# Filling a score operand stack in quarter-block portions, with the trailing attention stages one pair of steps closer

## The chip, the cores and the metric

The kernel runs on one core of one Trainium2 chip. The metric is the device time of one execution in microseconds (us). The kernel before takes 1998.75 us, the median of three runs (1997.51 to 2001.54).

## What is computed

Four layers of a Flamingo-like decoder in float32, on x of 8 x 256 tokens x 256 features, against a context of the same shape. Each layer is a gated cross-attention (16 heads of 16 features) followed by a gated feed-forward part; the latter differs from layer to layer (two dense ones in layer 0, eight experts with two chosen in layers 1 and 2, a quantised one with a convolution in layer 3). Cut to what matters here:

```
for l in range(4):
    x = x + tanh(g_xattn[l]) * xattn_l(norm(x), ctx)   # layer 0 with a mask of keys
    x = x + tanh(g_ffn[l]) * ffn_l(norm(x))
xattn: q, k, v = projections, heads of 16
       scores = q k^T / 4; attn = softmax(scores over keys); out = attn v
```

Only the attention of each layer is touched by the change.

## The kernel before

**Split operands.** To keep float32 accuracy, every query and key value is split into a high part and a low remainder. A score is the sum of three products, so the operands are stacked on partitions: `stack` holds, for each of two heads (partitions 0 and 64 on), three row blocks of 16 partitions: for the keys high, high, low; for the queries high, low, high. Partition 48 of each head holds one more row: ones for the keys, and for the queries the negated row maximum, so that the second score product comes out with the maximum already taken off. One slot of `stack` holds one block: one batch entry of 256 tokens, all eight pairs of heads. There are three slots (`SLOTS`) for eight blocks.

**How the stack is filled.** SyncE stores the split values of 512 tokens to the DRAM tensor `qk_parts` (`store_k`, `store_q`, three stores of 512 KB each, in the order of the row blocks), and GpSimd loads them back in stack form (`load_stack`: four loads of 48 x 8 x 256 values, 384 KB each, for one block: keys of two heads, queries of two heads). Both wait on counting semaphores: `k_out` and `q_out` say that a store has landed, `stack_in` of a slot that its loads have.

**The pipeline.** A step `t` is one pair of heads of one block; a turn `n` of the loops in `attend` is two steps (the code counts 32 turns as `QUADS`), so a block is four turns: block `b` begins with turn 4b. In turn n TensorE computes the natural scores of the turn (`scores_nat`, L792), VectorE takes their row maxima (`maximum`, L1709), and one turn later TensorE transposes the maxima (`max_rows`, L814), ScalarE copies them to `mt` (`take_rows`, L1294), and GpSimd writes them as a row into the stack by a small DMA (`put_rows`, L545). `KEY` turns after the natural scores TensorE computes the keyed scores (`scores_key`, L827) from stack and row, which ScalarE exponentiates (L1285); `TIMES_V` turns behind come the products with the values (L852), and `BACK` turns behind the transposes back (L865) and the divisions.

**What sets the order.** Every engine runs its program in order; there is no scheduler. In GpSimd's program the first three blocks are loaded ahead of the first turn, and `put_rows(l, n)` of turns 7, 11, 15, 19 and 23 is followed by the four loads of one later block. All these DMAs share GpSimd's queue and are served in the order in which they are issued. `mt` has two buffers, and ScalarE waits before it writes one again until the row written from it has landed:

```
if j >= 2:
    act.wait_ge(row_in[j % 2], 16 * (j // 2))
```

In TensorE's program the natural scores stand first in each turn, and the first of a block waits for the whole block; keyed scores, `max_rows`, `back` and `times_v` of that turn stand behind it:

```
if c == 0:
    loads = sum(x % SLOTS == b % SLOTS for x in range(B)) * l + b // SLOTS + 1
    pe.wait_ge(stack_in[b % SLOTS], 64 * loads + 16 * (l + 1))
```

Of the kernel before, what the change touches and what calls it, by code (L numbers as in the profile page):

```python
# [25 lines left out]
F32 = mybir.dt.float32  # L26
F32R = mybir.dt.float32r
# [8 lines left out]
P = 128  # L36
B, S, D = 8, 256, 256
# [13 lines left out]
STACK = 3 * DH + 1  # L51
MAXROW = 3 * DH
SLOTS = 3
KEY, TIMES_V, BACK = 4, 5, 6
PROJ_IN = {1: 48, 2: 80, 3: 128}
MASKED = -2.0 ** 100
MAGIC = 1.5 * 2.0 ** 23
# [36 lines left out]
def build(nc, io, upto=8):  # L94

    ctx = ExitStack()
    with ctx:
        def sb(name, shape, dt=F32, stack=ctx):
            return stack.enter_context(nc.sbuf_tensor(name, shape, dt))

        def sem(name, n=None):
            if n is None:
                return ctx.enter_context(nc.semaphore(name))
            return [ctx.enter_context(nc.semaphore(f"{name}{i}")) for i in range(n)]
# [48 lines left out]
        k_parts = sb("k_parts", [P, 2, 2, KC, 512], F32R, at)  # L153
        q_parts = sb("q_parts", [P, 2, 2, KC, 512], F32R, at)
        vpad = sb("vpad", [P, TILES, HEADS * (DH + 1) + 16], F32, at)
        mt = sb("mt", [8, 2, P], F32R, at)
        probs = sb("probs", [P, 4, 512], F32, at)
        pvs = sb("pvs", [P, 2, 256], F32, at)
        rc = sb("rc", [P, 2, 2, 4], F32, at)
# [1 line left out]
        def k_hi(g):  # L161
            return k_parts[:, g % 2, 0]

        def k_lo(g):
            return k_parts[:, g % 2, 1]

        def q_lo(g):
            return q_parts[:, g % 2, 0]

        def q_hi(g):  # L170
            return q_parts[:, g % 2, 1]
# [85 lines left out]
        xt = nc.dram_tensor("x_tokens", (T, D), F32, kind="Internal").ap()  # L257
        xs = nc.dram_tensor("xs_sorted", (NT * P, D), F32, kind="Internal").ap()
        ys = nc.dram_tensor("ys_sorted", (NT * P, D), F32, kind="Internal").ap()
        parts = nc.dram_tensor("qk_parts", (2, 2, MAXROW, PAIRS, T), F32, kind="Internal").ap()  # L260

        PS = ctx.enter_context(nc.psum_tensor("PS", [P, 8, 512], F32))

# [13 lines left out]
        qhi_done, qlo_done, v_done = sem("qhi_done"), sem("qlo_done"), sem("v_done")  # L277
        k_out, q_out = sem("k_out", 2), sem("q_out", 2)
        stack_in = sem("stack_in", SLOTS)
        mt_done, row_in = sem("mt_done"), sem("row_in", 2)  # L280
        nat_mm, max_done = sem("nat_mm"), sem("max_done")
        maxT_mm = sem("maxT_mm")
        sc_mm, exp_done = sem("sc_mm"), sem("exp_done")
# [46 lines left out]
        def stored(out, l, g):  # L330

            n = GROUPS * l + g
            return out[n % 2], 48 * (n // 2 + 1)

        def rows_of(n, r, g):

# [16 lines left out]
        def _(sp):  # L353
# [11 lines left out]
            def store_k(l, g):  # L365

                sp.wait_ge(khi_done, GROUPS * l + g + 1)
                sp.wait_ge(klo_done, GROUPS * l + g + 1)
                for r, part in enumerate((k_hi(g), k_hi(g), k_lo(g))):
                    sp.dma_start(rows_of(1, r, g), part.bitcast(F32)).then_inc(k_out[g % 2], 16)  # L370

            def store_q(l, g):

                sp.wait_ge(qhi_done, GROUPS * l + g + 1)
                sp.wait_ge(qlo_done, GROUPS * l + g + 1)
                for r, part in enumerate((q_hi(g), q_lo(g), q_hi(g))):
                    sp.dma_start(rows_of(0, r, g), part.bitcast(F32)).then_inc(q_out[g % 2], 16)

            def load_proj(l):
# [129 lines left out]
        def _(pool):  # L509
# [9 lines left out]
            def load_expert(l, e):  # L519
# [5 lines left out]
                nc.gpsimd.dma_start(wslot[:, slot, KC * h:2 * KC * h].rearrange("p (j d) -> p j d", d=D),  # L525
                                    io[f"W2_{l}"][e * h:(e + 1) * h, :].rearrange("(j p) d -> p j d", p=P)
                                    ).then_inc(w_in[slot], 16)
            def load_stack(l, b):

                if b >= SLOTS:  # L530
                    pool.wait_ge(sc_mm, 2 * STEPS * l + 2 * PAIRS * (b - SLOTS + 1))
                else:
                    nc.gpsimd.dma_start(stack[MAXROW:MAXROW + 65:64, b % SLOTS, 1].rearrange("p c n -> p (c n)"),
                                        io["ones_rows"]).then_inc(stack_in[b % SLOTS], 16)
                for n, out in ((1, k_out), (0, q_out)):
                    pool.wait_ge(*stored(out, l, b // 2))
                    for h in range(2):
                        nc.gpsimd.dma_start(stack[64 * h:64 * h + MAXROW, b % SLOTS, n],  # L538
                                            parts[n, h][:, :, b * S:(b + 1) * S]).then_inc(stack_in[b % SLOTS], 16)

            def put_rows(l, n):

                j, c, b = QUADS * l + n, 2 * n % PAIRS, 2 * n // PAIRS
                pool.wait_ge(mt_done, j + 1)
                nc.gpsimd.dma_start(stack[MAXROW:MAXROW + 65:64, b % SLOTS, 0, c:c + 2, :].rearrange("p c n -> p (c n)"),  # L545
                                    mt[:, j % 2, :]).then_inc(row_in[j % 2], 16)
            for l in lo_l:
                if l:

# [12 lines left out]
                if l == 0:  # L562

                    def make_mask(b):
                        pool.wait_ge(mask_in[b % 2], 32 * (b // 2 + 1))
                        nc.gpsimd.tensor_scalar(mask_b[:, b], stage_i[:, b % 2], 0.0, None, ALU.is_equal
                                                ).then_inc(mask_done, 1)
                    for g in range(GROUPS):

                        pool.wait_ge(khi_done, g + 1)  # L570
                        if g >= 2:
                            pool.wait_ge(*stored(k_out, 0, g - 2))
                        nc.gpsimd.tensor_tensor(k_lo(g), ctx_at(g), k_hi(g).bitcast(F32), ALU.subtract
                                                ).then_inc(klo_done, 1)
                        if g < 2:
                            make_mask(g)
                    load_stack(0, 0)
                    pool.wait_ge(v0_in, 16)
                    for g in range(GROUPS):
                        nc.gpsimd.tensor_copy(v_heads(4 * g, 4)[:, :, :, 0:DH],  # L580
                                              v_in[:, 4 * g:4 * g + 4, :].rearrange("p t (h d) -> p t h d", d=DH)
                                              ).then_inc(v_done, 1)
                else:
                    load_stack(l, 0)
                load_stack(l, 1)
                load_stack(l, 2)
                for n in range(QUADS):
                    if l == 0 and n % 2 == 1 and n // 2 + 2 < B:
                        make_mask(n // 2 + 2)
                    put_rows(l, n)  # L590
                    if n % 4 == 3 and n >= 7 and n // 4 + 2 < B:
                        load_stack(l, n // 4 + 2)
                if l == 3 and ffn(3):

                    pool.wait_ge(o_done, QUADS * 4)
# [75 lines left out]
        def _(pe):  # L671
# [102 lines left out]
            def scores_nat(l, t):  # L774

                s, b, c = STEPS * l + t, t // PAIRS, t % PAIRS
                if t == 0:
                    pe.wait_ge(qlo_done, GROUPS * (l + 1))
                    pe.wait_ge(klo_done, GROUPS * (l + 1))
                    if l:  # L780
                        pe.wait_ge(v_done, GROUPS * (l + 1))
                if c == 0:
                    loads = sum(x % SLOTS == b % SLOTS for x in range(B)) * l + b // SLOTS + 1
                    pe.wait_ge(stack_in[b % SLOTS], 64 * loads + 16 * (l + 1))
                if s:
                    pe.wait_ge(max_done, 2 * s - 1)
                q, kk = stack[:, b % SLOTS, 0, c], stack[:, b % SLOTS, 1, c]
                for qt in range(2):

                    for h in range(2):  # L790
                        rows = slice(64 * h, 64 * h + MAXROW)
                        mm = pe.matmul(PS[:, (2 * t + h) % 3, qt * S:(qt + 1) * S], q[rows, qt * P:(qt + 1) * P],  # L792
                                       kk[rows], start=(l > 0 or qt == 0), stop=(l > 0), skip_group_check=(l == 0))
                        if l and qt:
                            mm.then_inc(nat_mm, 1)
# [20 lines left out]
            def scores_key(l, t):  # L816

                s, b, c = STEPS * l + t, t // PAIRS, t % PAIRS
                j = s // 2
                pe.wait_ge(row_in[j % 2], 16 * (j // 2 + 1))  # L820
                if s:
                    pe.wait_ge(exp_done, 2 * s - 1)
                q, kk = stack[:, b % SLOTS, 0, c], stack[:, b % SLOTS, 1, c]
                for kt in range(2):
                    for h in range(2):
                        rows = slice(64 * h, 64 * h + STACK)
                        mm = pe.matmul(PS[:, 3 + (2 * t + h) % 3, kt * S:(kt + 1) * S], kk[rows, kt * P:(kt + 1) * P],  # L827
                                       q[rows], start=(l > 0 or kt == 0), stop=(l > 0), skip_group_check=(l == 0))
                        if l and kt:
                            mm.then_inc(sc_mm, 1)  # L830
# [367 lines left out]
        def _(act):  # L1198
# [89 lines left out]
            def take_rows(l, n):  # L1288

                j = QUADS * l + n  # L1290
                act.wait_ge(maxT_mm, j + 1)
                if j >= 2:
                    act.wait_ge(row_in[j % 2], 16 * (j // 2))
                nc.scalar.activation(mt[:, j % 2, :], PS[0:8, 6, S:S + P], ACT.Identity).then_inc(mt_done, 1)  # L1294

            def take_pv(l, n):

# [979 lines left out]
```

## Time and profile before

| | |
|---|---|
| median of three runs | 1998.75 us |
| the profiled execution | 1983.74 us |
| its span, first to last instruction | 1981.9 us |
| mean granted TensorE clock | 0.868 of full speed |
| TensorE busy | 1470.5 us, 74% |
| VectorE busy | 1083.2 us, 55% |
| ScalarE busy | 735.4 us, 37% |
| GpSimd busy | 544.0 us, 27% |

The profile is of one execution. Busy time is the union of an engine's instructions; the shares are averages over stages with different limits, so a stage must be looked at by itself. The four attention stages lie at about 56 to 255, 449 to 610, 1111 to 1268 and 1630 to 1802 us of the span. In rows of the time line the columns are start, duration, engine, line, operation and tiles, count, and in brackets how long the engine was idle before and what ended that.

### The profile page before, as it was taken

The numbers are of one execution on the slowest core, as the hardware profiler recorded it, in microseconds if no ns is written. First come the engines' busy times: TensorE is split into PE (matmuls) and PEld (weight loads), VectorE is DVE, ScalarE is ACT, GpSimd is POOL, SyncE is SP. The second block draws the span as 40 slices with busy tenths as digits, with TensorE's granted clock in tenths as the row PEclk, the third lists the DMA queues.
The fourth block names the chain that finished last, engine by engine and source line by source line (L and its number), as shares of the span: only waits on it lengthen the run. The fifth ranks groups of instructions, "written<-read, shape, count | busy, mean of one in ns | idle before, by whom it ended". The sixth has DMA issues, their size and how long they took to land.

```text
span 1981.9 us, 29494 instructions
## 1 busy us (share of the span) xinstructions
PE 1470.5 (74%) x9789; PEld 1035.4 (52%) x9816; DVE 1083.2 (55%) x2363; ACT 735.4 (37%) x1458; POOL 544.0 (27%) x519
## 2 busy tenths in 40 slices
PE   1489959986777349997996477942899755788676
PEld 1245548853445248887884244521788523455334
DVE  5256563346565515554537466581455556565797
ACT  2145644324555113332321255620344213554342
POOL 4342220021220353345315222007443431222000
PEclk9989979996789679998998688975999986779897
DMA  9989420099980241322126999012432593980000
GB/s 307 239 221 83 34 67 1 1 303 151 79 66 20 77 155 58 133 77 69 37 73 225 224 72 91 2 53 98 158 103 85 160 275 95 87 66 2 0 11 32
DMA packets 153868, 202.65 MB, mean 102 GB/s; under 512 B 19968, under 2 KB 113542, under 8 KB 153736
## 3 DMA queue, kind: packets, MB, share of 16 engines
q0 software_dynamic: 75392, 95.15, 33.7%
q1 hardware_dynamic: 78368, 106.05, 16.7%
q8 instruction: 69, 1.13, 0.3%
q14 instruction: 39, 0.32, 0.1%
HBM read 120.25 MB, written 80.35 MB: 101 GB/s over the span
## 4 chain that ended last, share of the span: by engine, by line
PE 48%; DMA 17%; DVE 15%; issue 8%; POOL 4%; ACT 4%; another core or an unknown queue 2%; SPq 2%; DVEq 0%; ACTq 0%; POOLq 0%
DMA stack<-mt 11%; PE PS L852 5%; PE PS L792 4%; PE PS L892 3%; PE PS L827 3%; PE PS L1030 2%; PE PS L1032 2%; PE PS L1031 2%; PE PS L1008 2%; PE PS L1009 2%; PE PS L1007 2%; PE PS L1018 2%; DVE xng L1583 2%; DVE amx L2139 1%
## 5 line engine op out<-in xcount | busy, mean ns | idle before, releaser
L1709 DVE TENSOR_REDUCE nm<-PS 128x2 f32<-128x512 f32 x512 | 336.8, 683 | 261.3 <-PE PS L792 165.5
L792 PE MATMUL PS<-stack 48*128 48x256 f32 x1024 | 154.9, 387 | 107.0 <-DVE nm L1709 56.4
L545 POOL DMA_DIRECT2D stack<-mt x128 | 70.0, 547 | 506.4 <-ACT mt L1294 505.8
L792 PEld LDWEIGHTS PS<-stack 48*128 48x128 f32 x1024 | 94.9, 228 | 204.8 <-DVE nm L1709 108.9
L1285 ACT ACTIVATE probs<-PS 128x512 f32<-128x512 f32 x256 | 139.0, 595 | 64.7 <-PE PS L835 31.8
L1285 ACT ACTIVATE xng<-PS 128x512 f32<-128x512 f32 x256 | 138.3, 591 | 46.6 <-PE PS L835 23.9
L852 PE MATMUL PS<-probs,vpad 128*32 128x256 f32 x1024 | 85.8, 462 | 71.3 <-ACT mt L1294 69.2
L827 PE MATMUL PS<-stack 49*128 49x256 f32 x1024 | 121.9, 319 | 19.7 <-DMA stack<-mt 15.2
L1031 PE MATMUL PS<-whi,hl 128*128 x468 | 133.2, 285 | 0.0
L1032 PE MATMUL PS<-wlo,hh 128*128 x468 | 133.2, 285 | 0.0
L1030 PE MATMUL PS<-whi,hh 128*128 x468 | 133.1, 284 | 0.0
L1385 ACT ACTIVATE hh<-PS 128x512 fp32r<-128x512 f32 x117 | 65.8, 596 | 180.3 <-PE PS L1018 152.0
L1380 ACT ACTIVATE hn<-PS 128x512 f32<-128x512 f32 x117 | 69.8, 598 | 168.5 <-PE PS L1009 138.2
L624 POOL TENSOR_TENSOR whi<-wslot,zero 128x4096 fp32r<-128x4096 f32 (+1 forms) x12 | 63.6, 5301 | 208.5 <-PE PS L1032 208.5
L1988 DVE TENSOR_TENSOR hl<-PS,hh 128x512 fp32r<-128x512 f32 x117 | 77.3, 687 | 66.7 <-ACT hh L1385 49.2
L827 PEld LDWEIGHTS PS<-stack 49*128 49x128 f32 x1024 | 93.1, 217 | 31.7 <-DMA stack<-mt 18.4
L1294 ACT ACTIVATE mt<-PS 8x128 fp32r<-8x128 f32 x128 | 32.4, 253 | 201.2 <-PE PS L814 107.8
L1982 DVE CAST of_e<-is_e 128x128 fp32r (+1 forms) x78 | 88.3, 1132 | 25.8 <-POOL wlo L626 16.0
L538 POOL DMA_DIRECT2D stack<-qk_parts x128 | 80.8, 638 | 60.7 <-DMA qk_parts<-q_parts 46.3
L665 POOL DMA_INDIRECT wslot<-ys_sorted,pos x64 | 62.0, 969 | 126.5 <-DMA ys_sorted<-yo 98.4
L1008 PE MATMUL PS<-whi,xl 128*128 x234 | 94.9, 405 | 0.0
L1007 PE MATMUL PS<-whi,xh 128*128 x234 | 94.7, 405 | 0.0
(289 smaller groups left out, 3394.8 us busy)
## 6 DMA issues: line engine op xcount, KB each, us to landing
stack<-qk_parts POOLq DMA_DIRECT2D x128, 384.0 KB, 10.4
qk_parts<-k_parts SPq DMA_DIRECT2D x48, 512.0 KB
qk_parts<-q_parts SPq DMA_DIRECT2D x48, 512.0 KB, 10.9
wslot<-W_dram POOLq DMA_DIRECT2D x16, 1024.0 KB, 8.9
ys_sorted<-yo SPq DMA_DIRECT2D x78, 128.0 KB, 1.7
wide<-ctxT_dram SPq DMA_DIRECT2D x16, 512.0 KB, 5.8
wslot<-W_dram POOLq DMA_DIRECT2D x16, 512.0 KB, 6.1
xg<-xs_sorted SPq DMA_DIRECT2D x62, 128.0 KB, 2.1
```

The source lines that it names most:

```text
L538: nc.gpsimd.dma_start(stack[64 * h:64 * h + MAXROW, b % SLOTS, n], parts[n, h][:, :, b * S:(b + 1) * S]).then_inc(stack_in[b % SLOTS], 16)
L792: mm = pe.matmul(PS[:, (2 * t + h) % 3, qt * S:(qt + 1) * S], q[rows, qt * P:(qt + 1) * P], kk[rows], start=(l > 0 or qt == 0), stop=(l > ...
L827: mm = pe.matmul(PS[:, 3 + (2 * t + h) % 3, kt * S:(kt + 1) * S], kk[rows, kt * P:(kt + 1) * P], q[rows], start=(l > 0 or kt == 0), stop=( ...
L852: mm = pe.matmul(PS[32 * strip:32 * strip + 32, 6, 0:S], vpad[:, 2 * b + kt, (DH + 1) * head:(DH + 1) * head + 32], probs_at(t, h)[:, kt * ...
L1007: pe.matmul(PS[:, 1 + h, :], xh[:, p, c, :], hi[:, w], start=False, stop=False)
L1008: pe.matmul(PS[:, 1 + h, :], xl[:, p, c, :], hi[:, w], start=False, stop=False)
L1030: pe.matmul(o, hh[:, j, :], hi[:, w], start=False, stop=False)
L1031: pe.matmul(o, hl[:, j, :], hi[:, w], start=False, stop=False)
L1032: mm = pe.matmul(o, hh[:, j, :], lo[:, w], start=False, stop=(j == nj - 1))
L1285: nc.scalar.activation(probs_at(t, h), PS[:, 3 + (2 * t + h) % 3, :], ACT.Exp, scale=SCALE).then_inc(exp_done, 1)
L1709: nc.vector.tensor_reduce(nm[:, j % 2, at:at + 2], PS[:, (2 * t + h) % 3, :].rearrange("p (q n) -> p q n", q=2), AX.X, ALU.max, negate=Tru ...
L1982: nc.vector.tensor_copy(of_e[:, q, :], is_e[:, ds(i, 1)].bitcast(F32).broadcast_to([P, P])).then_inc(e_done, 1)
```

## The change

Four edits go together. Only the two distinct parts (high and low) are stored to `qk_parts`, two stores for each group of 512 tokens and operand in place of three; the repeated row block of the stack is made by the loads instead. A block is loaded in four portions (keys of head 0, keys of head 1, queries of head 0, queries of head 1), each of two DMAs, one of 16 and one of 32 partitions (128 KB and 256 KB). Block 0 and the first portion of block 1 are loaded ahead of the first turn; after that every `put_rows` up to turn 26 is followed by one portion, in such an order that the four portions of block b follow the rows of turns 4b-5, 4b-4, 4b-3 and 4b-2. `mt` and `row_in` have four buffers, not two. And `KEY`, `TIMES_V`, `BACK` are 3, 4, 5, not 4, 5, 6.

```diff
-KEY, TIMES_V, BACK = 4, 5, 6
+KEY, TIMES_V, BACK = 3, 4, 5
...
-        mt = sb("mt", [8, 2, P], F32R, at)
+        mt = sb("mt", [8, 4, P], F32R, at)
...
-        parts = nc.dram_tensor("qk_parts", (2, 2, MAXROW, PAIRS, T), F32, kind="Internal").ap()
+        parts = nc.dram_tensor("qk_parts", (2, 2, 2 * DH, PAIRS, T), F32, kind="Internal").ap()
...
-            return out[n % 2], 48 * (n // 2 + 1)
+            return out[n % 2], 32 * (n // 2 + 1)
...
-                for r, part in enumerate((k_hi(g), k_hi(g), k_lo(g))):
+                for r, part in enumerate((k_hi(g), k_lo(g))):
...
-                for r, part in enumerate((q_hi(g), q_lo(g), q_hi(g))):
+                for r, part in enumerate((q_hi(g), q_lo(g))):
...
-            def load_stack(l, b):
-
-                if b >= SLOTS:
+            def load_stack(l, b, at):
+
+                of, h = (1, 0)[at // 2], at % 2
+                if at == 0 and b >= SLOTS:
                     pool.wait_ge(sc_mm, 2 * STEPS * l + 2 * PAIRS * (b - SLOTS + 1))
-                else:
+                if at == 0 and b < SLOTS:
                     nc.gpsimd.dma_start(stack[MAXROW:MAXROW + 65:64, b % SLOTS, 1].rearrange("p c n -> p (c n)"),
                                         io["ones_rows"]).then_inc(stack_in[b % SLOTS], 16)
-                for n, out in ((1, k_out), (0, q_out)):
-                    pool.wait_ge(*stored(out, l, b // 2))
-                    for h in range(2):
-                        nc.gpsimd.dma_start(stack[64 * h:64 * h + MAXROW, b % SLOTS, n],
-                                            parts[n, h][:, :, b * S:(b + 1) * S]).then_inc(stack_in[b % SLOTS], 16)
+                pool.wait_ge(*stored((q_out, k_out)[of], l, b // 2))
+                rows = lambda r, n: stack[64 * h + DH * r:64 * h + DH * (r + n), b % SLOTS, of]
+                part = parts[of, h][:, :, b * S:(b + 1) * S]
+                first, both = (0, 1) if of else (2, 0)
+                nc.gpsimd.dma_start(rows(first, 1), part[0:DH]).then_inc(stack_in[b % SLOTS], 16)
+                nc.gpsimd.dma_start(rows(both, 2), part).then_inc(stack_in[b % SLOTS], 16)
...
-                                    mt[:, j % 2, :]).then_inc(row_in[j % 2], 16)
+                                    mt[:, j % 4, :]).then_inc(row_in[j % 4], 16)
...
-                load_stack(l, 1)
-                load_stack(l, 2)
+                load_stack(l, 1, 0)
                 for n in range(QUADS):
                     if l == 0 and n % 2 == 1 and n // 2 + 2 < B:
                         make_mask(n // 2 + 2)
                     put_rows(l, n)
-                    if n % 4 == 3 and n >= 7 and n // 4 + 2 < B:
-                        load_stack(l, n // 4 + 2)
+                    if (n + 5) // 4 < B:
+                        load_stack(l, (n + 5) // 4, (n + 1) % 4)
...
-                    pe.wait_ge(stack_in[b % SLOTS], 64 * loads + 16 * (l + 1))
+                    pe.wait_ge(stack_in[b % SLOTS], 128 * loads + 16 * (l + 1))
...
-                if j >= 2:
-                    act.wait_ge(row_in[j % 2], 16 * (j // 2))
+                if j >= 4:
+                    act.wait_ge(row_in[j % 4], 16 * (j // 4))
```

GpSimd's program in the attention of layer 1, from the row of turn 0 to those of turns 8 to 11, before (L545 is `put_rows`, L538 a load of the stack; the row with x8 stands for the rows of eight turns, turns 0 to 7):

```order
L545 DMA stack<-mt 2x4x128 [waits mt_done] x8
L538 DMA stack<-qk_parts 48x8x256 [waits k_out1,sc_mm]
L538 DMA stack<-qk_parts 48x8x256
L538 DMA stack<-qk_parts 48x8x256 [waits q_out1]
L538 DMA stack<-qk_parts 48x8x256
L545 DMA stack<-mt 2x4x128 [waits mt_done] x4
```

and the same engine and layer now, from the rows of turn 0 to those of turn 3 (L547 is `put_rows`, L540 and L541 the two DMAs of a portion of block 1, L534 the first DMA of block 2):

```order
L547 DMA stack<-mt 2x4x128 [waits mt_done]
L540 DMA stack<-qk_parts 16x8x256 [waits k_out0]
L541 DMA stack<-qk_parts 32x8x256
L547 DMA stack<-mt 2x4x128 [waits mt_done]
L540 DMA stack<-qk_parts 16x8x256 [waits q_out0]
L541 DMA stack<-qk_parts 32x8x256
L547 DMA stack<-mt 2x4x128 [waits mt_done]
L540 DMA stack<-qk_parts 16x8x256 [waits q_out0]
L541 DMA stack<-qk_parts 32x8x256
L547 DMA stack<-mt 2x4x128 [waits mt_done]
L534 DMA stack<-ones_rows_dram 2x2048
```

The loads that stood in one piece of four between two rows stand now in pairs between all rows, and the last pair of block 1 stands behind the row of turn 2.

TensorE's program in layer 1 at turns 3 and 4, where the first keyed scores begin, before (L792 natural scores, L827 keyed scores, L814 `max_rows`; `stack_in1` is the wait for the whole of block 1, `row_in` that for a row):

```order
L792 MATMUL PS<-stack 128x256 [waits max_done]
L792 MATMUL PS<-stack 128x256 x3
L814 MATMUL PS<-ident,nm 128x128 [waits pv_done,mt_done,max_done]
L792 MATMUL PS<-stack 128x256 [waits max_done]
L792 MATMUL PS<-stack 128x256 x3
L792 MATMUL PS<-stack 128x256 [waits max_done,stack_in1]
L792 MATMUL PS<-stack 128x256 x3
L827 MATMUL PS<-stack 128x256 [waits exp_done,row_in0]
```

and now:

```order
L795 MATMUL PS<-stack 128x256 [waits max_done]
L795 MATMUL PS<-stack 128x256 x3
L830 MATMUL PS<-stack 128x256 [waits exp_done,row_in0]
L830 MATMUL PS<-stack 128x256 x3
L817 MATMUL PS<-ident,nm 128x128 [waits pv_done,mt_done,max_done]
L795 MATMUL PS<-stack 128x256 [waits max_done]
L795 MATMUL PS<-stack 128x256 x3
L830 MATMUL PS<-stack 128x256 [waits exp_done,row_in0]
L830 MATMUL PS<-stack 128x256 x3
L795 MATMUL PS<-stack 128x256 [waits max_done,stack_in1]
L795 MATMUL PS<-stack 128x256 x3
L830 MATMUL PS<-stack 128x256 [waits exp_done,row_in1]
```

The keyed scores begin one turn earlier. `max_rows` of turn 3 (L817) carries the maxima of turn 2, whose row GpSimd writes ahead of the last portion of block 1; the next turn's first natural scores wait for that portion.

## Rows read from the trace of the kernel before

**Rows 1.** The page's chain of work that ended last, its shares by line

```profile
DMA stack<-mt 11%; PE PS L852 5%; PE PS L792 4%; PE PS L892 3%; PE PS L827 3%; PE PS L1030 2%; PE PS L1032 2%; PE PS L1031 2%; PE PS L1008 2%; PE PS L1009 2%; PE PS L1007 2%; PE PS L1018 2%; DVE xng L1583 2%; DVE amx L2139 1%
```

**Rows 2.** Waits: engine and line, waited for, us in total, times, longest

```profile
ACT mt L1294 <- DMA stack<-mt: 93.4, 20, 13.8
```

**Rows 3.** Time line of GpSimd in the attention of layer 1

```profile
454.38 0.57 POOL L545 DMA_DIRECT2D stack<-mt  x1 [8.37 <-ACT mt L1294]
...
488.61 2.52 POOL L538 DMA_DIRECT2D stack<-qk_parts  x4
...
491.21 0.56 POOL L545 DMA_DIRECT2D stack<-mt  x1
...
502.81 0.53 POOL L545 DMA_DIRECT2D stack<-mt  x1 [7.91 <-ACT mt L1294]
...
507.30 0.53 POOL L545 DMA_DIRECT2D stack<-mt  x1 [3.95 <-ACT mt L1294]
...
512.29 0.56 POOL L545 DMA_DIRECT2D stack<-mt  x1 [1.95 <-ACT mt L1294]
...
597.15 0.53 POOL L545 DMA_DIRECT2D stack<-mt  x1 [2.37 <-ACT mt L1294]
```

**Rows 4.** Time line of TensorE in layer 1: starts of turns 9 and 10, and a wait

```profile
488.93 0.50 PE L792 MATMUL PS<-stack 48*128 48x256 f32 x4
...
492.07 0.50 PE L792 MATMUL PS<-stack 48*128 48x256 f32 x4
...
502.66 1.94 PE L852 MATMUL PS<-probs,vpad 128*32 128x256 f32 x16 [5.44 <-ACT mt L1294]
```

**Rows 5.** Issue to landing of row 488.08 and load 488.61, both of GpSimd

```profile
DMA to landing us min/median/max: 1.6/3.5/5.4
```

**Rows 6.** Windows of 1 us: busy of each engine, then granted clock, DMA share, GB/s

```profile
501.00:502.00 1.00, 0.00 (x0) 0.00 (x0) 0.00 (x0) 0.00 (x0) 0.00 (x0) 0.58 0.00 0
...
511.00:512.00 1.00, 1.00 (x11) 0.69 (x9) 0.80 (x3) 1.00 (x3) 0.00 (x0) 0.80 2.03 128
```

**Rows 7.** Time line of GpSimd in the attention of layer 0

```profile
80.91 0.57 POOL L545 DMA_DIRECT2D stack<-mt  x1 [21.50 <-ACT mt L1294]
...
190.20 0.56 POOL L545 DMA_DIRECT2D stack<-mt  x1 [4.12 <-ACT mt L1294]
...
237.09 0.53 POOL L545 DMA_DIRECT2D stack<-mt  x1 [3.48 <-ACT mt L1294]
```

**Rows 8.** Time line of TensorE, starts of two turns in layer 0

```profile
187.15 0.51 PE L792 MATMUL PS<-stack 48*128 48x256 f32 x4
...
191.83 0.50 PE L792 MATMUL PS<-stack 48*128 48x256 f32 x4
```

**Rows 9.** Time line of GpSimd, first and last rows of layers 2 and 3

```profile
1115.71 0.57 POOL L545 DMA_DIRECT2D stack<-mt  x1 [12.60 <-ACT mt L1294]
...
1255.20 0.53 POOL L545 DMA_DIRECT2D stack<-mt  x1 [2.37 <-ACT mt L1294]
...
1655.53 0.57 POOL L545 DMA_DIRECT2D stack<-mt  x1 [27.14 <-ACT mt L1294]
...
1789.37 0.53 POOL L545 DMA_DIRECT2D stack<-mt  x1 [2.25 <-ACT mt L1294]
```

**Rows 10.** Time lines of VectorE at the start of the attention, layers 0 and 3

```profile
75.47 1.29 DVE L1709 TENSOR_REDUCE nm<-PS 128x2 f32<-128x512 f32 x2 [35.02 <-DMA iotas<-iotas_dram]
...
1647.02 2.29 DVE L1816 TENSOR_REDUCE q<-wslot 128x1 f32<-128x2048 f32 x1 [16.68 <-DMA wslot<-W_dram]
```

**Rows 11.** The page's DMA issues: count, KB each, us to landing

```profile
qk_parts<-q_parts SPq DMA_DIRECT2D x48, 512.0 KB, 10.9
```

**Rows 12.** One window of 2 us before the attention of layer 0

```profile
64.00:66.00 2.00, 0.00 (x0) 0.00 (x0) 0.00 (x0) 0.00 (x0) 0.00 (x0) 1.00 1.19 367
```

**Rows 13.** Time line of TensorE in the last turns of layer 1

```profile
601.29 0.44 PE L865 MATMUL PS<-ident,pvs 128*128 128x128 f32 x2
...
604.01 0.44 PE L865 MATMUL PS<-ident,pvs 128*128 128x128 f32 x2
```

More of the change, by code:

```diff
@@ L279, in build @@
         stack_in = sem("stack_in", SLOTS)
-        mt_done, row_in = sem("mt_done"), sem("row_in", 2)
+        mt_done, row_in = sem("mt_done"), sem("row_in", 4)
         nat_mm, max_done = sem("nat_mm"), sem("max_done")
@@ L576, in _ @@
                             make_mask(g)
-                    load_stack(0, 0)
+                    for at in range(4):
+                        load_stack(0, 0, at)
                     pool.wait_ge(v0_in, 16)
@@ L583, in _ @@
                 else:
-                    load_stack(l, 0)
-                load_stack(l, 1)
-                load_stack(l, 2)
+                    for at in range(4):
+                        load_stack(l, 0, at)
+                load_stack(l, 1, 0)
                 for n in range(QUADS):
@@ L819, in scores_key @@
                 j = s // 2
-                pe.wait_ge(row_in[j % 2], 16 * (j // 2 + 1))
+                pe.wait_ge(row_in[j % 4], 16 * (j // 4 + 1))
                 if s:
@@ L1291, in take_rows @@
                 act.wait_ge(maxT_mm, j + 1)
-                if j >= 2:
-                    act.wait_ge(row_in[j % 2], 16 * (j // 2))
-                nc.scalar.activation(mt[:, j % 2, :], PS[0:8, 6, S:S + P], ACT.Identity).then_inc(mt_done, 1)
+                if j >= 4:
+                    act.wait_ge(row_in[j % 4], 16 * (j // 4))
+                nc.scalar.activation(mt[:, j % 4, :], PS[0:8, 6, S:S + P], ACT.Identity).then_inc(mt_done, 1)
             def take_pv(l, n):
```

## Prediction

> **What bounds the kernel now.** I read the page's chain of waits first: one line of small transfers, `stack<-mt`, 4 KB each, holds 11% of the span [rows 1]. The list of waits says who waits for them: ScalarE before it overwrites `mt`, 93.4 us over 20 places [rows 2]. Behind that wait stand the exponentials, behind them everything else.
>
> The time line of GpSimd in layer 1 shows why. A turn takes 3.14 us when nothing waits: the natural scores of turns 9 and 10 start at 488.93 and 492.07 [rows 4]. At 488.61 four loads (1.5 MB) are issued; the row of turn 8, at 491.21, stands behind them in the queue, ScalarE needs its `mt` buffer back for turn 10, and the row of turn 10 comes 7.91 us of idle time later, at 502.81 [rows 3]. The next turns take 4.49 and 4.99 us, not 3.14 [rows 3]: TensorE's granted clock fell from 2.4 to 1.2 GHz at about 501.4, late in its idle time, and rose again at about 511.4 [rows 6].
>
> So the attention stages are worth reading as 31 turns between the row of turn 0 and that of turn 31, plus excess. In layers 1 to 3 the 31 turns are 31 x 3.14 = 97.3 us. Layer 1 takes 597.15 - 454.38 = 142.8 [rows 3], layers 2 and 3 139.5 and 133.8 [rows 9]: excess 45.5, 42.2 and 36.5, in sum 124. In layer 0, whose mask products make a turn 191.83 - 187.15 = 4.68 us [rows 8], the rows span 156.2 us [rows 7], excess 11. The change attacks these 135 us.
>
> **What the change takes away: all of it.** `mt` has four buffers, and a row has only one portion ahead of it, issued 3.14 - 0.56 = 2.6 us earlier. A load of 384 KB lands 5.4 us after its issue, a row with nothing ahead of it in 1.6 [rows 5]; so the row lands some 3 us after its issue. Its keyed scores begin two turn boundaries later, 0.86 + 3.14 = 4.0 us after it (0.86 is worked out below). I count the old excess, 124 + 11 = 135 us, as gone.
>
> **What it adds: a new wait, in TensorE's own queue.** Before, block 3, first needed in turn 12, was issued in turn 8, at 488.61 [rows 3]. Now the last portion of block b follows the row of turn 4b-2, and that row exists only once turn 4b-1 is under way, since its maxima are transposed there. The next turn, 4b, begins with natural scores that wait for the whole block, and in TensorE's queue everything stands behind them: keyed scores, `max_rows`, the value products; VectorE, ScalarE and GpSimd run dry within a turn.
>
> The size, from layer 1: the row of turn 8 is issued at 491.21, the next turn's natural scores start at 492.07 [rows 3, 4], so a turn boundary comes 0.86 us after a row's issue. The portion is issued 0.56 us after the row [rows 3] and lands 5.4 us after that if it behaves as one 384 KB load [rows 5]. Wait: 0.56 + 5.4 - 0.86 = 5.1 us. Bounds of the landing: a second issue may cost its full 0.6 us (2.52 us for four, rows 3) on top, 6.0; and nothing can land sooner than the 1.6 us of a 4 KB row. I take 5.4, since the bytes and queue are the same. In layer 0 the row at 190.20 is followed by the next turn's start at 191.83 [rows 7, 8], 1.63 us later: 0.56 + 5.4 - 1.63 = 4.3 us.
>
> The clock comes on top. An idle stretch like this one, the 5.44 us before 502.66, halved it [rows 4, 6], and the two turns after cost (4.49 - 3.14) + (4.99 - 3.14) = 3.2 us [rows 3]. Bounds: nothing if the clock holds, 4 x 1.85 = 7.4 if a whole block stays at 1.2 GHz. I take 3.2; in layer 0, with no row of its own, 2.0 between 0 and 3.2.
>
> There are seven such boundaries in each layer (blocks 1 to 7), also at blocks 1 and 2, which had none before. Layers 1 to 3: 21 x (5.1 + 3.2) = 174; layer 0: 7 x (4.3 + 2.0) = 44. Together 218 us against 135 removed: **+83 us**.
>
> On one point a rule of the Trainium skill can be weighed against these rows. The row says 5.4 us from issue to landing for 384 KB [rows 5]. The page "DMA: Bandwidth & Descriptors", section "Anatomy of one DMA — SWDGE (gpsimd) path", fits such a transfer as about 2.0 us plus the bytes at 436 GB/s, an estimate of 2.9 us; the trace disagrees. By it the wait would be 2.6 us and the whole sum about 28 x 2.5 = 70 us lower.
>
> **The start of each layer, -31 us.** Ahead of layer 0's attention the DMA engines are full (367 GB/s at 64 us [rows 12]), and VectorE's second start waits until 75.47 for a constant queued behind all stores [rows 10]. Of its 24 stores of 512 KB [rows 11] eight go: 4.2 MB at 367 GB/s is 11.4 us, and seven of the twelve portions loaded ahead compete no longer. I take 14, between 8 and 20. In layer 3 VectorE idles 16.68 us until 1647.02 for weights that stand behind the query stores and beside the same loads [rows 10]; four stores fewer give 4 x 1.4 = 5.7 us, no competing loads up to the 16.7: I take 12. Layers 1 and 2 load block 0 beside their query stores; four of them fewer are at most 5.7 us each, and I take 2.5 each, 5 in sum. Bounds of the whole: 20 to 45.
>
> **The end of each layer, -7 us.** One trailing turn fewer: 604.01 - 601.29 = 2.7 us [rows 13] in layers 1 to 3, some 3.5 in layer 0, together 12; but turn 3 now carries keyed scores at the halved clock, which costs 1 to 1.5 us each.
>
> GpSimd issues 256 DMAs for the portions, not 128: at about 0.6 us some 75 us more, hidden in its idle time before rows (2.4 to 4.1 us a turn [rows 3, 7]), where one portion takes 1.25. If that cover were gone, rows would come later by as much; it is not.
>
> **Sum:** +83 - 31 - 7 = +45 us: from the profiled execution's 1983.7 us to 2029, and from the median, which lies 15 us above that execution, to **2044 us**.
>
> **Rivals.**
> - *The clock holds through the waits (13%).* The new idle stretch of 5.1 us is close to the 5.44 us in which the clock fell, which speaks against; for it speaks that the clock fell only at about 501.4, with 1.3 us of that stretch to go [rows 4, 6]. Then 21 x 3.2 + 7 x 2.0 = 81 us less: 1963, faster than before.
> - *A portion lands much sooner than 5.4 us (10%).* Two smaller DMAs might be served side by side. Each us off the landing is worth 28 us; the sign turns at 1.6 us, a landing of 3.8 us. At 3.2 us: 2044 - 62 = 1982. Against it: bytes, run length of 1 KB and queue are as in rows 5. This is also where the skill's rule would lead.
> - *The new wait doesn't exist (4%):* portions land within 0.86 us, or TensorE lags so far that it doesn't notice. Then 135 + 31 + 7 = 173 us less, 1826. Speaks for it only a misread order; 1.6 us is the fastest landing seen.
> - *The waits are longer or the clock stays halved for most of a block (5%):* at 6.0 us of landing and 4.5 us of clock cost 28 x 0.6 + 21 x 1.3 = 44 more, 2088.
>
> **How the numbers follow.** The forecast as such has 68%; its own range, with landings of 5.1 to 6.0, 2.6 to 3.8 us of clock cost and 20 to 45 us at the starts, is 2010 to 2078. For 8 in 10 the range goes down to the first rival, 1963, and up to 2078; the fourth and fifth case and half of the second lie outside. About 0.2% is what a measurement of this kernel can tell from no change. Slower: the forecast and the last rival, less a tail, 72%; faster: the first and third rival, most of the second, 25%; the same: 3%.
>
> **What the profile after would show.** Right: L795 on TensorE idle about 5 us before turns 4, 8, ... 28 with `stack<-qk_parts` as releaser; a landing of 5 to 6 us after a portion's first DMA; L1294 no longer waiting for `stack<-mt`; rows of turns 0 to 31 about 155 us apart in layers 1 to 3 (before 134 to 143); the clock at 1.2 GHz after each boundary; layer 0 starting before 65 us. Wrong: four even turns of 3.14 us across a boundary, or boundaries with the clock at 2.4 GHz.

## The result, and the profile after

The changed kernel is slower by about 0.65%: 2007.98 us, the median of seven runs, against 1994.32 us for the kernel before, now the median of seven runs too, a ratio of 1.0065 (95% interval 1.0047 to 1.0083). On another chip, where both are some 3% faster, it was 1.0061 (1.0037 to 1.0084). The forecast had the sign and the mechanism, but more than three times the size: +45 us (2044) was forecast, +13.7 us was measured.

The profiled execution of after has a span of 2005.8 us, 23.9 us more than that of before. The page's chain of waits names another tile than before [rows 1], and the list of waits another engine [rows 2]:

```profile
DMA stack<-qk_parts 7%; PE PS L795 7%; PE PS L855 6%; PE PS L830 3%; PE PS L895 3%; PE PS L1033 2%; PE PS L1035 2%; PE PS L1034 2%; PE PS L1011 2%; PE PS L1012 2%; PE PS L1010 2%; PE PS L1021 2%; DVE nm L1712 2%; PE PS L805 2%
```

```profile
PE PS L795 <- DMA stack<-qk_parts: 154.6, 31, 18.4
```

ScalarE's wait for rows is gone, and TensorE's natural scores wait for a block's load. The boundary to turn 8 in layer 1, on TensorE's time line (L855, the value products, ends the turn before):

```profile
491.72 1.07 PE L855 MATMUL PS<-xng,vpad 128*32 128x256 f32 x16
...
497.02 0.79 PE L795 MATMUL PS<-stack 48*128 48x256 f32 x4 [4.24 <-DMA stack<-qk_parts]
...
502.02 0.79 PE L795 MATMUL PS<-stack 48*128 48x256 f32 x4
...
507.02 0.79 PE L795 MATMUL PS<-stack 48*128 48x256 f32 x4
```

Turn 8 starts at 497.02 after a wait of 4.24 us; turns 9 and 10 follow at 5.00 us each, the length of a turn at 1.2 GHz, where 3.14 is that at 2.4 [rows 4]. GpSimd's time line of the same layer, with the first and last rows, and the row and the portion ahead of that boundary:

```profile
465.69 0.56 POOL L547 DMA_DIRECT2D stack<-mt  x1 [10.75 <-ACT mt L1297]
...
491.86 0.56 POOL L547 DMA_DIRECT2D stack<-mt  x1 [1.50 <-ACT mt L1297]
492.41 0.53 POOL L540 DMA_DIRECT2D stack<-qk_parts  x1
492.93 0.57 POOL L541 DMA_DIRECT2D stack<-qk_parts  x1
...
613.68 0.53 POOL L547 DMA_DIRECT2D stack<-mt  x1 [2.37 <-ACT mt L1297]
```

The time from issue to landing of the two DMAs of that portion, its minimum that of the first, its maximum that of the second:

```profile
DMA to landing us min/median/max: 3.6/3.8/4.1
```

The second, issued at 492.93, lands 4.1 us later, at 497.0, and TensorE starts at 497.02: 4.6 us after the portion's first issue. The granted clock in windows of 1 us (third figure from the end) falls in the wait and rises again 14 us later:

```profile
494.00:495.00 1.00, 0.00 (x0) 0.00 (x0) 0.00 (x0) 0.00 (x0) 0.00 (x0) 0.71 1.44 200
508.00:509.00 1.00, 1.00 (x12) 0.64 (x8) 1.00 (x2) 0.74 (x2) 0.00 (x0) 0.97 1.15 96
```

The first and last rows in the other layers (layer 0, then 2, then 3), and VectorE at the start of layers 0 and 3:

```profile
68.25 0.56 POOL L547 DMA_DIRECT2D stack<-mt  x1 [14.35 <-ACT mt L1297]
...
252.98 0.53 POOL L547 DMA_DIRECT2D stack<-mt  x1 [3.47 <-ACT mt L1297]
...
1131.04 0.56 POOL L547 DMA_DIRECT2D stack<-mt  x1 [17.52 <-ACT mt L1297]
...
1276.44 0.53 POOL L547 DMA_DIRECT2D stack<-mt  x1 [2.37 <-ACT mt L1297]
...
1668.58 0.56 POOL L547 DMA_DIRECT2D stack<-mt  x1 [39.37 <-ACT mt L1297]
...
1815.34 0.53 POOL L547 DMA_DIRECT2D stack<-mt  x1 [2.47 <-ACT mt L1297]
```

```profile
62.81 1.29 DVE L1712 TENSOR_REDUCE nm<-PS 128x2 f32<-128x512 f32 x2 [22.57 <-DMA iotas<-iotas_dram]
...
1660.07 2.29 DVE L1819 TENSOR_REDUCE q<-wslot 128x1 f32<-128x2048 f32 x1 [11.02 <-DMA wslot<-W_dram]
```

From row of turn 0 to row of turn 31, before [rows 3, 7, 9] and after:

| layer | before, us | after, us | turns alone, us |
|---|---|---|---|
| 0 | 156.2 | 184.7 | 145.1 |
| 1 | 142.8 | 148.0 | 97.3 |
| 2 | 139.5 | 145.4 | 97.3 |
| 3 | 133.8 | 146.8 | 97.3 |
| sum | 572.3 | 624.9 | 437.0 |

The rows stretch costs 52.6 us more. All that lies between these stretches costs 28.7 us less: 12.7 ahead of layer 0's first row (80.91 to 68.25), 4.6 and 1.2 between the layers 0, 1 and 2, 8.2 between 2 and 3, 2.0 behind.

### The profile page after: what moved, and what is told of

The parts are those of the page before. It is cut to its first block, busy times and chain, and to the rows that moved or that the text cites. A ratio compares the mean times of both kernels' runs of the same rounds, so it can differ in the third digit from the quotient of the medians.

```text
span 2005.8 us, 29614 instructions
## 1 busy us (share of the span) xinstructions
PE 1491.0 (74%) x9815; PEld 1050.4 (52%) x9816; DVE 1085.5 (54%) x2363; ACT 735.0 (37%) x1458; POOL 604.8 (30%) x647
## 4 chain that ended last, share of the span: by engine, by line
PE 57%; DVE 13%; DMA 10%; issue 7%; POOL 5%; ACT 4%; another core or an unknown queue 2%; SPq 1%; DVEq 0%; ACTq 0%; POOLq 0%
DMA stack<-qk_parts 7%; PE PS L795 7%; PE PS L855 6%; PE PS L830 3%; PE PS L895 3%; PE PS L1033 2%; PE PS L1035 2%; PE PS L1034 2%; PE PS L1011 2%; PE PS L1012 2%; PE PS L1010 2%; PE PS L1021 2%; DVE nm L1712 2%; PE PS L805 2%
## 5 line engine op out<-in xcount | busy, mean ns | idle before, releaser
L795 PE MATMUL PS<-stack 48*128 48x256 f32 x1024 | 160.5, 400 | 193.7 <-DMA stack<-qk_parts 154.6
L547 POOL DMA_DIRECT2D stack<-mt x128 | 71.3, 557 | 498.0 <-ACT mt L1297 498.0
L1034 PE MATMUL PS<-whi,hl 128*128 x468 | 133.8, 286 | 0.0
L830 PEld LDWEIGHTS PS<-stack 49*128 49x128 f32 x1024 | 99.4, 232 | 10.9 <-issue 10.3
L1012 PE MATMUL PS<-wlo,xh 128*128 x234 | 95.1, 406 | 0.0
L1033 PEld LDWEIGHTS PS<-whi,hh 128*128 128x128 f32 x468 | 91.2, 195 | 0.0
L1034 PEld LDWEIGHTS PS<-whi,hl 128*128 128x128 f32 x468 | 91.0, 195 | 0.0
```

The costliest lines, as they stand in the source:

```text
L1012: mm = pe.matmul(PS[:, 1 + h, :], xh[:, p, c, :], lo[:, w], start=False, stop=(c == KC - 1))
L1033: pe.matmul(o, hh[:, j, :], hi[:, w], start=False, stop=False)
L1034: pe.matmul(o, hl[:, j, :], hi[:, w], start=False, stop=False)
```

## The experiments

The runs below are of four chips, so ratios are to the kernel before on the same chip. Before takes 1996.8 us on the chip of e1 to e4 (the first chip below); on the chips of e5 to e8, of e9 to e11 and of e12 it takes 1938.1, 1938.1 and 1938.5 us. "Rows" are the stretches of the table above.

**Distance alone** (`e1_key3_alone`), the kernel before with one line changed:

```diff
-KEY, TIMES_V, BACK = 4, 5, 6
+KEY, TIMES_V, BACK = 3, 4, 5
```

> The kernel before with only KEY, TIMES_V, BACK = 3, 4, 5. Theory A (the boundary waits for the last portion are the whole loss): this has no such waits; one trailing turn less in each layer gives 5 to 12 us, the old waits for rows stay, so 1983 to 1990 us against 1994, ratio 0.995 to 0.998. Theory B (the loss comes from the shorter distance: keyed scores now meet rows that have not landed): slower than before by 10 us or more, ratio 1.005 or above, with TensorE L827 waiting for stack<-mt at more places than the 13 of before.

Measured: 2029.93 us, ratio 1.0168 (1.0138 to 1.0198). My expectation missed, its Theory B holds for this kernel: TensorE's keyed scores meet rows that stand behind four loads. In layer 1, turn 11:

```profile
520.16 0.80 PE L827 MATMUL PS<-stack 49*128 49x256 f32 x4 [6.71 <-DMA stack<-mt]
```

The row of turn 8, issued at 508.95 behind four loads, lands 11.2 us later, as before (11.0); but now TensorE itself waits for it, since its keyed scores need it in turn 11, one turn sooner than before, where ScalarE waited.

**Distance put back** (`e2_key4_portions`), the changed kernel with that line as before:

> The changed kernel with KEY, TIMES_V, BACK back at 4, 5, 6. Theory A: the boundary waits stay as they are (4.2 to 4.6 us each in layers 1 to 3) and one trailing turn comes back, so 5 to 12 us above the changed kernel: 2013 to 2020 us. Theory B: the changed kernel's loss goes, 1985 to 1995 us.

Measured: 2020.21 us, ratio 1.0111 (1.0084 to 1.0138), against 1.0065 for the changed kernel: at the upper edge of what Theory A had (2013 to 2020). The boundary waits of layers 1 to 3 are still there, 4.2 to 5.1 us. Theory B falls for the changed kernel: in it the shorter distance is worth about 9 us (1.0111 less 1.0065, of 1997), though it costs 33 us by itself. The edits do not add up one by one: a row that has one portion ahead of it can afford the shorter distance, a row behind four loads cannot.

**Portions two turns earlier** (`e3_two_turns_earlier`):

```diff
-                load_stack(l, 1, 0)
+                for at in range(3):
+                    load_stack(l, 1, at)
...
-                    if (n + 5) // 4 < B:
-                        load_stack(l, (n + 5) // 4, (n + 1) % 4)
+                    if (n + 7) // 4 < B:
+                        load_stack(l, (n + 7) // 4, (n + 3) % 4)
```

> The changed kernel with each portion issued two turns earlier (three portions of block 1 ahead of the first turn; the last portion of block b behind the row of turn 4b-4). Theory A: the boundary has 0.86 + 2 x 3.14 us of cover for a landing of 5.2 us after the row, so all 28 waits and their clock loss go: the rows of turns 0 to 31 span 97 to 108 us in layers 1 to 3 (148, 145 and 147 in the changed kernel) and 145 to 155 in layer 0 (181), together 150 to 185 us less, 1825 to 1860 us. Theory C (GpSimd's queue cannot carry a portion of 2.5 us and a row in 3.14 us, the waits only show it): waits move to the rows, and less than 60 us is gained.

Measured: 1840.20 us, ratio 0.9216 (0.9192 to 0.9240), as Theory A had it; Theory C falls. The rows of layer 1:

```profile
433.10 0.56 POOL L547 DMA_DIRECT2D stack<-mt  x1 [9.07 <-ACT mt L1298]
...
535.22 0.54 POOL L547 DMA_DIRECT2D stack<-mt  x1 [2.37 <-ACT mt L1298]
```

102.1 us, and 148.0, 101.5 and 99.7 in layers 0, 2 and 3: 451.3 in sum, 14 above the bare turns (the changed kernel has 624.9). No boundary waits any more, but for 0.4 us at one, and most of the 14 us lie in the first five turns of a layer. GpSimd carries a portion and a row in each turn of 3.14 us.

**Portions one turn earlier** (`e5_one_earlier`), the same edit with `range(2)`, `(n + 6) // 4` and `(n + 2) % 4`:

> The changed kernel with each portion one turn earlier (two portions of block 1 ahead of the first turn). Theory A (the wait is the landing of the last portion less its cover): cover 0.86 + 3.14 = 4.0 us against a landing about 5.2 us after the row's issue, so 1.2 us left at a boundary of layers 1 to 3 and none in layer 0, too short to halve the clock: rows of turns 0 to 31 span 107 to 115 us in layers 1 to 3, total 1850 to 1875 us. Theory C (the queue is the bound): waits of more than 3 us stay, 1900 us or more.

Measured: 1815.94 us against 1938.10, ratio 0.9373 (0.9348 to 0.9397). That is less in absolute time than was written because of the chip; by the ratio it is 1872 of 1997. The boundary waits of layers 1 to 3 are 1.1 to 2.8 us, on average 28.2 / 21 = 1.34, where the changed kernel has 4.45: 3.1 us less, just one turn. The boundary to turn 16:

```profile
493.38 0.50 PE L796 MATMUL PS<-stack 48*128 48x256 f32 x4 [1.12 <-DMA stack<-qk_parts]
```

and the matmul runs in 0.50 us, at 2.4 GHz. The clock fell behind 4 of these 21 waits, not behind none as was written. The rows span 113.8, 113.0 and 109.2 us. In layer 0 a wait of 1.7 us is left at one of seven boundaries. With 4.45, 1.34 and none left at the three positions, the wait is the landing less its cover, in amount too.

**One DMA of 48 partitions for a portion** (`e6_one_dma_of_48`), with the three stores it needs:

```diff
-                nc.gpsimd.dma_start(rows(first, 1), part[0:DH]).then_inc(stack_in[b % SLOTS], 16)
-                nc.gpsimd.dma_start(rows(both, 2), part).then_inc(stack_in[b % SLOTS], 16)
+                nc.gpsimd.dma_start(stack[64 * h:64 * h + MAXROW, b % SLOTS, of],
+                                    parts[of, h][:, :, b * S:(b + 1) * S]).then_inc(stack_in[b % SLOTS], 16)
```

> The changed kernel with the three stores of before and each portion as one DMA of 48 partitions (384 KB). If the 5.4 us of such a load in the trace of before hold, the boundary wait of layers 1 to 3 is 5.1 us, not the 4.3 measured with two DMAs, and each boundary costs 0.7 to 1.0 us more with the clock: 20 to 28 us; the starts give back another 15 to 30 us: 2043 to 2066 us. Rival (the shape of the DMA does not matter, the landing of before was long because three more loads stood behind it): boundary wait 4.2 to 4.4 us, only the starts are lost, 2023 to 2038 us.

Measured: 1980.56 us, ratio 1.0220 (1.0192 to 1.0247), just under my range (1.023 as a ratio). It lies between the two theories. The landing of the row and the portion ahead of turn 12 of layer 1, and TensorE's wait there:

```profile
DMA to landing us min/median/max: 2.7/3.8/5.0
```

```profile
535.13 0.80 PE L792 MATMUL PS<-stack 48*128 48x256 f32 x4 [4.66 <-DMA stack<-qk_parts]
```

A load of 384 KB lands in 5.0 us, not in the 5.4 of [rows 5]; as two DMAs it lands in 4.6. The 21 waits are 4.79 us on average. So about half of the 0.8 us by which I had the landing too long comes from the shape. The other half is in the traces too: over the 15 places of layers 1 to 3, the first of four loads in before lands after 5.3 us (median; the one in rows 5 is longer than most), and in e7 and e9, which issue four portions in one piece, the first portion lands after 4.9 where one by itself takes 4.6. With three more issued right behind it a load lands 0.3 us later, in either shape.

**Four `mt` buffers alone** (`e4_mt4_alone`), the kernel before with the edits of the diff on `mt` and `row_in`:

> The kernel before with only four buffers of mt (and four row_in semaphores). ScalarE no longer waits; TensorE's keyed scores of turn 8 (in turn 12, due about 498.8 us in layer 1) still wait for the row landing at 502.2. Theory A: each of the 15 stalls of layers 1 to 3 shrinks from about 5 to 3 to 3.5 us, some no longer halve the clock: 20 to 50 us less, 1945 to 1975 us. Rival: the row's landing is what counts, whoever waits for it, and nothing changes (within 6 us of before).

Measured: 1955.57 us, ratio 0.9799 (0.9760 to 0.9837), inside Theory A's range, though by another wait than was written: past the start of a layer no keyed scores wait for a row. The rows span 132.4, 125.2 and 122.5 us in layers 1 to 3. What is left at block 3 of layer 1 is TensorE's wait for that block's own load, since turn 12 now comes sooner:

```profile
501.42 0.80 PE L792 MATMUL PS<-stack 48*128 48x256 f32 x4 [2.76 <-DMA stack<-qk_parts]
```

**All but the portions** (`e7_burst_rest_after`), the changed kernel with its four portions issued in one piece after the rows of turns 7, 11, ..., as before had its loads:

```diff
-                    if (n + 5) // 4 < B:
-                        load_stack(l, (n + 5) // 4, (n + 1) % 4)
+                    if n % 4 == 3 and n >= 7 and n // 4 + 2 < B:
+                        for at in range(4):
+                            load_stack(l, n // 4 + 2, at)
```

> The changed kernel with the portions of a block issued in one piece where before had them (after the rows of turns 7, 11, ... and three blocks ahead of the first turn); two stores, four mt buffers and KEY = 3 stay. Theory A: no boundary waits, but the row of turn 8 lands 11 us after its issue and the keyed scores of turn 11 need it 4.0 us after: 6 to 7 us wait in TensorE at five places and one of 10 us or more at the start, each with the halved clock: 60 to 66 us excess in layers 1 to 3, so 2015 to 2045 us, no better than the portions as they are. Rival (the portions are what hurts, anything else is better): below 1990 us.

Measured: 1947.15 us, ratio 1.0043 (1.0022 to 1.0063); by it 2005 us on the first chip, a little below my range. A row behind four portions lands 7.4 to 9.1 us after its own issue, not 11, because the eight issues keep GpSimd 4.4 us and the row is itself issued later. At the five loads within layer 1 the keyed scores wait 4.7 to 6.4 us, not 6 to 7, and the rows span 150.9, 151.7 and 137.7 us. The first of them:

```profile
507.71 0.80 PE L833 MATMUL PS<-stack 49*128 49x256 f32 x4 [5.33 <-DMA stack<-mt]
```

The rival falls: with the shorter distance the loads in one piece are no better than the portions as they are, 1.0043 to 1.0065 or 1.0061, with intervals that overlap.

**Stores and DMAs alone** (`e9_stores_and_dmas_only`), the same with two `mt` buffers and `KEY` 4:

> Of the change only the two stores for three and the loads as pairs of DMAs of 16 and 32 partitions; issued in one piece as before, two mt buffers, KEY 4. The starts gain: layer 0 by 8 to 15 us, layer 3 by 5 to 14, layers 1 and 2 by 1 to 5 each, 15 to 35 us in all; the waits of ScalarE for rows stay within 1 us each unless the pairs of DMAs are faster than single ones (then a row lands up to 3 us sooner behind four portions, and up to 50 us go): 1960 to 1980 us, or 1930 to 1960 with faster pairs.

Measured: 1905.36 us against 1938.13, ratio 0.9850 (0.9817 to 0.9884), 33 us less; by the ratio 1967 us on the first chip, in the first of the two ranges. Against a trace of before on the same chip the rows gain 11 us in sum (564.1 against 575.1), the starts and the rest 21. The pairs are a little faster, not 3 us: a row behind four portions lands 12.7 us after the first of their issues, in before behind four loads 13.4 (medians of 15).

**Two turns earlier, two `mt` buffers** (`e8_two_earlier_mt2`) **or `KEY` 4** (`e10_two_earlier_key4`):

> The version with portions two turns earlier (1840 us) and the two mt buffers of before. A row lands some 3 us after its issue and its buffer is wanted again 6.3 us after it: ScalarE should never wait and the time should be the same, 1835 to 1846 us. Rival: rows behind portions are late often enough that ScalarE waits, more than 1855 us.

> The version with portions two turns earlier and KEY, TIMES_V, BACK = 4, 5, 6. With no waits left the distance only costs its trailing turn: 2.7 us in each of layers 1 to 3 and 3.5 in layer 0, less 1 to 1.5 us each at the start: 5 to 12 us more than 1840, 1845 to 1852. Rival: rows at a distance of three turns are sometimes late, and four turns are faster, below 1838.

Measured: 0.9146 (0.9120 to 0.9172) and 0.9237 (0.9213 to 0.9260). The absolute times, 1775.29 and 1788.55 us, are of faster chips; by the ratios they are 1826 and 1844 us on the first, 9 us under what was written for e8 and at the lower edge for e10. In rows, e3 has 451.3 us in sum, e8 453.8: the four buffers are of no use once no burst of loads stands ahead of a row. The ratio of e8 lies under e3's 0.9216, but it is from another chip, where the stages outside attention are shorter: it saves 163 us there, e3 157 on the first. `KEY` 4 saves 150 us on the chip of e10, 13 us less than `KEY` 3 with two buffers on that of e8, near the 5 to 12 us expected for the trailing turns. Their two traces don't show this difference (spans of 1779.0 and 1778.7 us).

**Both kernels once more** (`e11_before_again`, one execution, and `e12_changed_again`):

> The kernel before once more, for a second trace of it. Its profiled execution took 1983.7 us, less than any of its timed runs (1990.6 to 2001.5). If its attention waits vary from run to run, the span of the rows of turns 0 to 31 in layers 1 to 3 differs from 142.8, 139.5 and 133.8 us by several us here; rival: the attention spans are the same within 2 us and the difference lies in other stages.

> The changed kernel once more, for a second trace and a second ratio. By the first pair of traces it loses 23.9 us, by the timed runs 13.7. If the waits at the boundaries are fixed by the landing of a portion, its rows of turns 0 to 31 span 148, 145 and 147 us in layers 1 to 3 again (within 3 us each) and the ratio to before comes out between 1.005 and 1.013; rival: the spans move by 5 us or more and the ratio changes sign.

The attention of before repeats within 3 us a layer: 154.3, 142.0, 142.2 and 136.6 us of rows, 575.1 in sum against 572.3. So does that of the changed kernel: 185.2, 145.6, 146.9, 149.6, 627.3 in sum against 624.9. The ratio is 1.0061. What differs is the rest: outside the rows this pair of traces, which are of two chips, shows 45.7 us less for the changed kernel, the first pair 28.7. So the +23.9 us of the first pair and the +6.5 of the second (1941.8 less 1935.3) lie on either side of the timed 9 to 14 us. Where outside attention an execution gains or loses these 10 us was not found.

## Why the prediction was wrong

**The step that failed is the size of the boundary term**, 21 x (5.1 + 3.2) + 7 x (4.3 + 2.0) = 218 us against 135 removed. What stands above the bare turns measured 624.9 - 437.0 = 188 us. Its parts:

- *The wait.* The 21 waits in the trace of after sum to 93.4 us, 4.45 each, where 5.1 was forecast (107); the seven of layer 0 sum to 28.0, 4.0 each, where 4.3 was forecast (30). That is 16 us of the error. The landing was read off the first of four loads in one piece (5.4 us), and the portion, two smaller DMAs with nothing behind them, lands in 4.6 us (e6 shows that 0.4 us of this come from the shape). The forecast's own range took landings of 5.1 to 6.0 us; 4.6 lies below it, and what lay lower I had left to a rival.
- *The clock.* What is left of the 188 us after the waits, 148.3 - 93.4 = 54.9 us in layers 1 to 3, is 2.6 us a boundary, not 3.2, and 1.7 us in layer 0, not 2.0: 15 us of the error. The 3.2 came from a single place. In the trace of after the clock rises again sooner at many places: it stays at 1.2 GHz for some 7 us at 13 of the 18 later boundaries of layers 1 to 3, where before had 10 us behind that place, and behind a boundary follows one row at 4.1 to 5.1 us and then, at 5 of 21 places only, a second slow one. The 2.6 is a mean of unlike places: 2.75 us at the 18 later boundaries, 0.9 at the first of each layer, where the clock was at 1.2 GHz already before the wait (in layer 1 from 460.3 to 484.2 us), and 1.0 us in turn 2 of each layer.

**What held.** The removed 135 us, nearly: with the boundary waits gone (e3) the rows come within 14 us of the bare turns, most of it at the start of the layers. Those 14 us stand in the changed kernel too, so of the 135 some 121 went, and what the boundaries themselves cost is nearer 174 us (624.9 - 451.3) than 188; the difference of the two terms is the same. The order argument, that the block's last portion hangs on the last row but one and all of TensorE's queue on it, is in the trace as written, 28 times of 28, and one turn of distance is one turn of wait (e5, e3). The starts and ends were forecast at -38 us and measured -28.7 and -45.7 in the two pairs of traces, -37 on average; with 17 us between the pairs, that the average meets the forecast is partly luck. In layer 0 VectorE's start came 12.7 us sooner (14 forecast), in layer 3 its wait for the weights fell from 16.68 us [rows 10] to 11.02, and 8.2 us were gained between the layers where 12 plus the end of layer 2 were forecast.

So the sum, remade with what was measured, is 188 - 135 - 37 = +16 us, next to the timed +13.7. It is the mean of what the two pairs of traces lose, +23.9 and +6.5, and no surer than they are.

**The rivals.** The clock did not hold: it fell at the 18 later boundaries of layers 1 to 3 and at all seven of layer 0, at the first boundary of layers 1 to 3 it was low already, and at all 21 the next row comes 4.1 to 5.1 us behind, a slow turn. Ahead of 497.02 the clock fell some 1.6 us after TensorE fell idle (492.8 to 494.4). In before it fell at 501.2 rather than at the 501.4 that the prediction reads from a share of 0.58 [rows 6], 3.9 us into the idle stretch. The second rival, a portion that lands sooner, was the true direction, though by 0.8 us and not by the 2.2 it was priced at. The rule of the Trainium skill's page "DMA: Bandwidth & Descriptors" that was weighed there (section "Anatomy of one DMA — SWDGE (gpsimd) path"; about 2.0 us plus the bytes at 436 GB/s, for the second DMA of a portion, 256 KB, an estimate of 2.6 us) is not borne out either: that DMA takes 4.1 us.

**The edits, apart.** Two stores and paired DMAs alone: -1.5%. Four `mt` buffers alone: -2.0%. The shorter distance alone: +1.7%, in the changed kernel about -0.5%. Portions where they were put, against the loads in one piece with all else changed (e7): no gain, 1.0065 against 1.0043. In layers 1 to 3 they take from TensorE's keyed scores waits of 3.6 to 6.6 us at five places of a layer, and of 11 to 12 at the start of layers 1 and 2, and give its natural scores waits of 4.2 to 5.2 us at seven. All four edits with the portions two turns earlier: -8%.

## What to carry to other kernels

Cutting a burst of transfers into portions between small urgent ones shortens the wait behind the burst, but it also moves the last portion towards its reader: count from the issue of the last portion to the first instruction that needs the whole, and start the portions that much earlier. Here one turn of lead removed 3.1 us at each of the 21 places of layers 1 to 3 and the whole wait at six of the seven of layer 0, two turns all but 0.4 us of it at all 28, and the kernel then took 157 us less than before's 1997. An edit's price depends on its neighbours: the same shorter distance cost 33 us in the kernel before, with its loads in one piece, and gained 9 in the changed kernel, with its portions.

## What the runs showed of the hardware that was not expected

- A load of 48 x 8 x 256 float32 (384 KB in runs of 1 KB) from DRAM on GpSimd's queue lands 5.3 us after its issue with three such loads behind it (median of 15 in before), 5.0 alone (e6), and 4.6 (from the first issue, after) as two DMAs of 16 and 32 partitions, 4.9 with three such portions behind (e7, e9).
- Short waits of TensorE went with a fall of the granted clock too: in e4 it fell at 13 of 15 waits of 0.9 to 3.7 us for a block's load, in e5 at 4 of 21 waits of 1.1 to 2.8 us. What sets the two apart was not tested.
- The profiled execution of before was 10.6 us under the median of the timed runs (1983.7 against 1994.3), while its attention rows agree within 3 us in sum with those of its second trace, on another chip (572.3 and 575.1).
- Between chips the same kernels differ by 3% (1996.8 us for before on one, 1938.1, 1938.1 and 1938.5 on three others). In the two traces of before nearly all of it lies outside attention: from the last row of layer 1 to the first of layer 2 518.6 us in one, 486.7 in the other.
